# Router gathers paced by TensorE's progress, with the last three batches behind all expert tiles

## The reference, cut to what matters

```python
h = (x_flat @ W_gat).reshape(M, HEADS, NUM_EXPERTS)
e = leaky_relu(a_src[src] + a_dst[dst])            # per edge and head
ee = exp(e - segment_max(e, dst)[dst])
denom = segment_sum(ee, dst)
agg = segment_sum(h[src] * (ee / denom[dst])[:, :, None], dst)
topk_s, topk_i = top_k(layernorm(agg).mean_over_heads, 2)
w = softmax(topk_s)
for ei in range(4):                                # every expert for every node
    g = where(topk_i == ei, w, 0).sum(-1)
    out = out + g * (gelu(x @ W1[ei] + b1[ei]) @ W2[ei] + b2[ei])
```

## Time and profile before

| | |
|---|---|
| runs, median (lowest to highest) | 4270.76 us (4270.12 to 4277.53) |
| profiled execution, span | 5331.2 us |
| block 3, first matmul to the add of tile 99 | 2841.8 to 4967.6 us |
| POOL busy, whole span | 2832.6 us (53%) |
| PE busy, whole span | 3564.3 us (67%) |
| DVE busy, whole span | 2082.9 us (39%) |

### The profile page before, as it was taken

The page is one execution under the profiler, slowest core; times in us unless marked ns, Lnnn a source line. Parts: engine busy times, 40 slices in busy tenths (PEclk is TensorE's granted clock), DMA queues, the critical chain, the costliest instruction groups (busy, mean ns, idle before and its releaser), DMA issues. The chain is left out here.

```text
span 5331.2 us, 46344 instructions
## 1 busy us (share of the span) xinstructions
PE 3564.3 (67%) x12937; PEld 2313.0 (43%) x12938; DVE 2082.9 (39%) x4892; ACT 801.1 (15%) x1970; POOL 2832.6 (53%) x2937
## 2 busy tenths in 40 slices
PE   0688888888757777777626377768685777789200
PEld 0455555555445455555413154444453454455100
DVE  5456655665546555544311020211111120212378
ACT  5111211111101111111101011111111111112000
POOL 2666666666666666666655623653636444630420
PEclk9889899998878888888767588888787788899655
DMA  7444444444445555555512111211112111211387
GB/s 250 128 109 115 112 111 112 112 115 112 112 111 148 138 153 154 162 152 152 125 33 61 18 49 28 58 38 48 35 50 43 44 48 36 60 50 48 118 254 253
DMA packets 381413, 540.57 MB, mean 101 GB/s; under 512 B 120314, under 2 KB 297818, under 8 KB 381143
## 3 DMA queue, kind: packets, MB, share of 16 engines
q0 software_dynamic: 119136, 234.44, 20.0%
q1 hardware_dynamic: 243119, 288.12, 16.8%
q10 hardware_dynamic: 19016, 16.48, 0.9%
HBM read 392.03 MB, written 146.74 MB: 101 GB/s over the span
## 5 line engine op out<-in xcount | busy, mean ns | idle before, releaser
L788 POOL DMA_INDIRECT rows<-xn_rows,gsrc x1664 | 1606.6, 965 | 908.5 <-issue 459.8
L1357 POOL DMA_INDIRECT nb<-route_rows,idx x1024 | 1000.3, 977 | 897.7 <-DVE msg L1432 480.9
L1093 PE MATMUL PS<-rows,oh 128*128 128x257 f32 x3328 | 910.0, 427 | 351.9 <-issue 220.0
L1686 PE MATMUL PS<-arena,hid 128*125 128x256 f32 x3200 | 865.1, 422 | 408.5 <-issue 298.6
L1686 PEld LDWEIGHTS PS<-arena,hid 128*125 128x125 f32 x3200 | 662.9, 209 | 621.3 <-issue 502.6
L1093 PEld LDWEIGHTS PS<-rows,oh 128*128 128x128 f32 x3328 | 693.8, 214 | 488.8 <-issue 296.6
L1621 DVE TENSOR_TENSOR y_sb<-PS,b_b 125x512 f32<-125x512 f32 x200 | 128.7, 685 | 1781.4 <-remote 975.2
L1678 PE MATMUL PS<-x2g,arena 128*128 128x500 f32 x1600 | 722.6, 610 | 147.3 <-issue 94.0
L1678 PEld LDWEIGHTS PS<-x2g,arena 128*128 128x128 f32 x1600 | 313.5, 197 | 541.6 <-issue 473.0
L1647 ACT ACTIVATE hid<-PS,b_sb 128x500 f32<-128x500 f32 x400 | 269.9, 677 | 1109.9 <-PE PS L1678 688.9
L1165 PE MATMUL PS<-own_w,p_t 128*125 128x512 f32 x400 | 231.2, 662 | 77.7 <-ACT s_t L1053 54.5
(11 more groups left out here) (304 smaller groups left out, 3086.8 us busy)
## 6 DMA issues: line engine op xcount, KB each, us to landing
y_rows<-y_sb SPq DMA_DIRECT2D x100, 512.0 KB
arena<-y_rows SPq DMA_DIRECT2D x100, 512.0 KB
rows<-xn_rows,gsrc POOLq DMA_INDIRECT x1664
nb<-route_rows,idx POOLq DMA_INDIRECT x1024
sum_rows<-kept SPq DMA_DIRECT2D x104, 128.5 KB
x_rows<-x SPq DMA_DIRECT2D x100, 128.0 KB
hid<-x_rows SPq DMA_DIRECT2D x100, 128.0 KB
m_in<-sum_rows SPq DMA_DIRECT2D x100, 125.5 KB
```

Source lines behind the costliest of these rows:

```text
L788: pool.indirect_dma_start(out=rows[w][h][:, q, 0:D], out_offset=None, in_=xn_rows, in_offset=bass.IndirectOffsetOnAxis(ap=gsrc[:, s * HU + ...
L1093: last = mm(SUM[:, 0:D + 1], oh[w][h][:, q, :], rows[w][h][:, q, :], start=h == 0 and q == 0, stop=h == 1 and q == HU - 1)
L1357: pool.indirect_dma_start(out=nb[b % NBUF][:, c, :], out_offset=None, in_=route_rows, in_offset=bass.IndirectOffsetOnAxis(ap=idx[:, b * W ...
L1686: last = mm(Y[j % 2][e // 2][0:NP, (e % 2) * D:(e % 2 + 1) * D], hid[:, 4 * e + k, j * NP:(j + 1) * NP], w2_sb[:, e, k, :], start=k == 0, ...
```

## The change

Four things change together.

1. unit_after spaces the batches at 7 tiles in place of 5.65. scores(0) moves from tile 8 to 12, scores(12) from tile 76 to 96, and batches 13, 14 and 15 (LATE) get no tile: their scores and records stand behind the add of tile 99, one batch after the other.
2. Every fourth gather of a batch (SPREAD) also waits until TensorE has come to tile (b + c/64) * 7 + 1, told by s_hp in a group's first half and by s_y in its second (where_pe_is). From tile 100 on there is no such wait: the last one is that of column 8 in batch 14, which waits for 99 tiles.
3. The lane chain and its two transposes stand behind everything, no longer between tiles. The exps move with them.
4. SyncE stores the records of the late batches after it has issued the last stage's first eight tiles of loads.

```diff
@@ -49,6 +49,8 @@
 FG = NT // FT
 AHEAD = 4
 REST = 16
+SPREAD = 4
+TILES_A_BATCH = 7
 EVEN = 112
 NS = 2 * SPANS
 MIX_AT = NT + 3
@@ -150,8 +152,16 @@
 
 def unit_after(b):
 
-    t = int((b + 1) * 5.65) + 3
+    t = int((b + 1) * TILES_A_BATCH) + 3
     return t if t % 4 < 2 else t + 4 - t % 4
+
+
+def where_pe_is(tiles):
+
+    group, rest = int(tiles // 4), tiles % 4
+    if rest < 2:
+        return 0, group * 16 + int(rest * 8) + 1
+    return 1, group * 4 + int((rest - 2) * 2)
 
 
 def build(nc, x, src, dst, gnn_w, gnn_b, wqkv, wkv_t, wout_t, bout, w_gat, att_src, att_dst,
@@ -1285,8 +1295,7 @@
             s_out = [ev(f"s_out{q}") for q in range(AR)]
 
             batches_after = lambda t: [b for b in range(NB) if unit_after(b) == t]
-            LAST = unit_after(NB - 1)
-            assert LAST + 4 < NT and LAST // 4 == NG - 2
+            LATE = [b for b in range(NB) if unit_after(b) > NT - 4]
 
             @block.sync
             def _(sp):
@@ -1300,6 +1309,11 @@
                         sp.wait_ge(s_hp, (g - 1) * 16)
                     for i in range(4):
                         sp.dma_start(x2g[u][:, :, i, :], x2_turned[4 * g + i].rearrange("p (k n) -> p k n", k=2)).then_inc(s_x2l[u], 16)
+
+                def store_records(b):
+                    sp.wait_ge(s_rec, b + 1)
+                    sp.dma_start(rec_rows[0:EF, :].rearrange("(p f) c -> p f c", p=P)[:, b * W:(b + 1) * W, :],
+                                 rec[b % 2][:]).then_inc(s_recs[b % 2], 16)
 
                 load_group(0)
                 load_group(1)
@@ -1309,9 +1323,7 @@
                     sp.wait_ge(s_yc, t + 1)
                     sp.dma_start(y_rows[t], y_sb[t % 2][:]).then_inc(s_ys[t % 2], 16)
                     for b in batches_after(t - 2):
-                        sp.wait_ge(s_rec, b + 1)
-                        sp.dma_start(rec_rows[0:EF, :].rearrange("(p f) c -> p f c", p=P)[:, b * W:(b + 1) * W, :],
-                                     rec[b % 2][:]).then_inc(s_recs[b % 2], 16)
+                        store_records(b)
                     if t % 4 == 0 and t // 4 + 2 < NG:
                         load_group(t // 4 + 2)
 
@@ -1332,6 +1344,8 @@
                     sp.wait_ge(s_ys[u], 16 * NT // 2)
                 for t in range(YR):
                     final_loads(t)
+                for b in LATE:
+                    store_records(b)
                 for t in range(YR, NT):
                     final_loads(t)
                 for q in range(AR):
@@ -1349,6 +1363,10 @@
                     if b >= NBUF:
                         pool.wait_ge(s_nbf, b - NBUF + 1)
                     for c in range(W):
+                        at = (b + c / W) * TILES_A_BATCH + 1
+                        if c % SPREAD == 0 and at < NT:
+                            which, count = where_pe_is(at)
+                            pool.wait_ge((s_hp, s_y)[which], count)
                         if (b or c) and c % REST == 0:
                             for q in range(AHEAD):
                                 pool.wait_ge(s_nb[q], (b * W + c) // AHEAD * 16)
@@ -1627,9 +1645,11 @@
                         records(b)
                     for b in batches_after(t):
                         scores(b)
-                    for part, at in ((lane_ends, 1), (over_lanes, 2), (lane_sums, 3), (first_maxima, 4), (first_records, 5)):
-                        if t == LAST + at:
-                            part()
+                for b in LATE:
+                    scores(b)
+                    records(b)
+                for part in (lane_ends, over_lanes, lane_sums, first_maxima, first_records):
+                    part()
                 for k in range(FG):
                     weigh(k)
                     for t in range(k * FT, (k + 1) * FT):
@@ -1649,9 +1669,11 @@
                         for b in batches_after(4 * g + j):
                             act.wait_ge(s_dif, b + 1)
                             a(dd[:], dd[:], ACT.Exp).then_inc(s_ex, 1)
-                    if g == LAST // 4:
-                        act.wait_ge(s_endd, 1)
-                        a(dc[:], dc[:], ACT.Exp).then_inc(s_ende, 1)
+                for b in LATE:
+                    act.wait_ge(s_dif, b + 1)
+                    a(dd[:], dd[:], ACT.Exp).then_inc(s_ex, 1)
+                act.wait_ge(s_endd, 1)
+                a(dc[:], dc[:], ACT.Exp).then_inc(s_ende, 1)
                 act.wait_ge(s_fixd, 1)
                 a(d4[:], d4[:], ACT.Exp).then_inc(s_fixe, 1)
                 for k in range(FG):
@@ -1686,16 +1708,6 @@
                                 last = mm(Y[j % 2][e // 2][0:NP, (e % 2) * D:(e % 2 + 1) * D], hid[:, 4 * e + k, j * NP:(j + 1) * NP],
                                           w2_sb[:, e, k, :], start=k == 0, stop=k == 3)
                         last.then_inc(s_y, 1)
-                        if isinstance(g, int) and 4 * g + j == LAST + 2:
-                            pe.wait_ge(s_ends, 1)
-                            for k in range(4):
-                                last = nc.tensor.transpose(HP[0][0:20, k * P:(k + 1) * P], ends[:, k, :], ident)
-                            last.then_inc(s_endt, 1)
-                            pe.wait_ge(s_endc, 1)
-                        if isinstance(g, int) and 4 * g + j == LAST + 3:
-                            pe.wait_ge(s_fx, 1)
-                            nc.tensor.transpose(HP[1][:, 0:20], fm[:, 0:P], ident[0:20, 0:20])
-                            nc.tensor.transpose(HP[1][:, 20:40], fx[:, 0:P], ident[0:20, 0:20]).then_inc(s_back, 1)
 
                 for g in range(2):
                     group(g, g, 0)
@@ -1704,6 +1716,14 @@
                         group(i * 2 + (2 + u), u, i + 1)
                 for g in range(NG - 3, NG):
                     group(g, g % 2, g // 2)
+                pe.wait_ge(s_ends, 1)
+                for k in range(4):
+                    last = nc.tensor.transpose(HP[0][0:20, k * P:(k + 1) * P], ends[:, k, :], ident)
+                last.then_inc(s_endt, 1)
+                pe.wait_ge(s_endc, 1)
+                pe.wait_ge(s_fx, 1)
+                nc.tensor.transpose(HP[1][:, 0:20], fm[:, 0:P], ident[0:20, 0:20])
+                nc.tensor.transpose(HP[1][:, 20:40], fx[:, 0:P], ident[0:20, 0:20]).then_inc(s_back, 1)
 
 
 _INS = ["x", "src", "dst", "L0_gnn_weight", "L0_gnn_bias", "L0_mix_Wqkv", "kv_turned", "out_turned", "L0_mix_bout",
```

## The result

The changed kernel takes 4325.37 us (median of four runs, 4318.19 to 4328.70), the kernel before 4270.44 beside it. The ratio is 1.0122, 95% interval 1.0108 to 1.0137: some 52 us slower (55 between the two medians). The forecast had the sign right, and 4360 us.

What follows compares the result with a forecast made beforehand. POOL's chain of gathers was taken to bound the kernel, with about 100 us of slack on TensorE. Tiles -101 and tail +192 gave +91 on the median of 4271, about 4360 us; range 4315 to 4445.

Steps and rivals of the forecast that it cites:

- hold: Expert block: TensorE crawls beside bursts of gathers without a semaphore wait; seen in the first profile, predicted absent in runs.
- TensorE's slack: Expert tiles: TensorE alone needs less time than POOL's chain of gathers; about 100 us.
- The first rival: Expert block: unpaced gathers hold TensorE in the runs too, so the change is faster, about 3740 us; chance 0.11.
- the second: Graph stage: gathers are quicker in runs than in the trace, TensorE already bounds; about 4440 us; chance 0.12.
- the third: Paced gathers: the pace costs POOL more than its slack; 4560 us; chance 0.04.
- the fourth: Whole kernel: it comes out even, a hold of 190 us or so in the runs all goes; 4270 us; chance 0.05.
- the bounds worked out from rows, +83 and +100: Whole change: the sum with gathers at 1.394 us apart (+83) or 1.375 us (+100) instead of 1.385.
- the forecast's own 4330 to 4400: Whole kernel: range for the main case, POOL's chain as bound; chance 0.68.
- -101: Expert tiles: done 1402 us behind the first gather in place of 1503, as TensorE no longer waits for the router.
- +192: Tail: weigh(0) starts 217 us behind tile 99's add, where before it started 25.2 behind.
- 1.385 us a gather: Route gathers: interval between gathers in a burst, 87.2/63, used to price all 1,024 gathers.
- The sum of 4267: Kernel before: run time built from rows with POOL alone setting the pace, 2401 + 1420 + 82.8 + 363.6, against median 4270.8.

Runs made afterwards that it cites:

- e1: The kernel before, unchanged, profiled a second time: 4276.68 us, with a span of 4274.9 us.
- e2: The changed kernel without POOL's waits for TensorE, spacing of 7 tiles and late batches kept: 4240.17 us, 0.9918 of the kernel before.
- e8: The kernel before, unchanged, profiled a third time: 4273.46 us, with a span of 4271.7 us.
- e6: The changed kernel at spacing 5.65, no late batch, with the wait for TensorE on every gather instead of every fourth: 4303.52 us, ratio 1.0075.
- e4: The kernel before without the waits for all gathers to land ahead of every sixteenth: 4138.70 us, ratio 0.9687.

## Why the prediction was right, and where its size was wrong

The bound, the sign and the mechanism stand: no hold in the runs, the tiles gain TensorE's slack, the tail pays more. The first rival (a hold in the runs) fell with e1, e2 and e8, the second (quicker gathers in the runs) with e1, which lasts as long as a run, has gathers of 0.944 us and lets TensorE wait for the router, the third with e6, the fourth with the result. That 4325 lies in the stated range is owed to its margin: the bounds worked out from rows, +83 and +100, are 4354 and 4371, and the forecast's own 4330 to 4400 misses it by 5. The balance of terms, e1 against the changed kernel:

| step | as predicted | measured |
|---|---|---|
| tiles, to the add of tile 99 | -101 (1503 to 1402, from the first gather) | -148.5 (1540.8 to 1392.3, from the first matmul) |
| tile 99 to batch 15 landed | 161 | 173.4 |
| batch 15's scores and records | 13.8 | 13.7 |
| lane chain to first result gather | 12.9 | 12.7 |
| first result gather to weigh(0) | 28.9 | 26.2 |
| tile 99 to weigh(0), less before | +192 | +200.8 (225.9 less 25.1) |
| weigh(0) to the end | unchanged | -1.6 |
| sum, with -0.7 at the start | +91 | +50.0 (4324.9 less 4274.9) |

The runs differ by 52 to 55 us and these two executions by 50, since e1 lasted 6 us longer than the median of the kernel before that stood beside the changed one.

**The step that was mis-sized is the -101.** TensorE's own need was right to about a microsecond (1402 less 8.6 from the first gather to the first matmul is 1393.4, measured 1392.3). What was too short is POOL's chain in the kernel before, against which it was set: 1420 us from the first gather to batch 15's first scores instruction, where e1 has 1469.6 (2390.3 to 3859.9). The price of 1.385 us a gather was taken from a burst of 64, whose 63 intervals hold three rests; a batch has four, the fourth ahead of the next batch's first gather. So 1,024 gathers at that price hold 49 rests, and the kernel has 63; at 2.15 us the missing 14 are 30 of the 50 us. What is left is spread over later landings, longer rests and long gathers (below).

**Why the check against the median didn't show it.** The sum of 4267 lay within 0.1% of the median, and the prediction took that for proof. It was luck: by e1's rows its parts were off by up to 51 us and cancelled.

| part | in the sum | e1 |
|---|---|---|
| 1,663 graph gathers' intervals | 2079 | 2119.7 |
| last graph gather to first route gather | 192 | 140.6 |
| first route gather to batch 15's scores | 1420 | 1469.6 |
| scores to tile 99's add | 82.8 | 80.5 |
| that add to the end | 363.6 | 334.6 |

The first used the median duration of a gather, 0.946 us; the mean in e1 and in the changed kernel is 0.970, since some are longer. The second and the last were lengths read from the disturbed execution: the stretch of the earlier trace rows from weigh(0) to the end, 338.3 us, takes 309.5 in e1 and 307.9 in the changed kernel, with the same instructions. So stretches without route gathers were taken for undisturbed, and the first profile was disturbed there as well; the earlier trace rows show it for weigh(0).

**The tail's 12 us.** The prediction had 120 gathers at 1.385 us from 8.3 us ahead of the last add. POOL came some 6 us late to them (the first starts at 3789.93; 2.9 us of this is one gather of 3.86 us, at 3782.02), and its waits for landings were longer while the last stage's first loads ran. From POOL's timeline, the stretches on both sides of 3820, and the chain that ended last (start, us, what):

```profile
3782.02 3.86 POOL L1375 DMA_INDIRECT nb<-route_rows,idx  x1 [0.30 <-issue]
...
3806.03 0.94 POOL L1375 DMA_INDIRECT nb<-route_rows,idx  x1 [5.72 <-DMA nb<-route_rows,idx]
...
3790.00:3820.00 30.00, 0.00 (x0) 0.00 (x0) 14.10 (x40) 0.63 (x1) 17.22 (x18) 0.54 0.75 241
3820.00:3960.00 140.00, 0.00 (x0) 0.00 (x0) 13.14 (x38) 0.63 (x1) 95.89 (x101) 0.50 0.12 16
...
3799.36 5.88 DMA nb<-route_rows,idx
...
3826.77 2.35 DMA nb<-route_rows,idx
```

A gather lands after 5.88 us in the stretch in which DMA moves 241 GB/s, and after 2.35 in the one with 16 GB/s. The prediction had named those loads as issued "long before" and didn't ask what they run beside. That they cause the late landings is read from these rows alone; no run moved them.

## What to carry to other kernels

Compare a profile's span with the runs before reading a stretch of it; if it is far off, take a second profile before any term. A sum that meets the median is a test only when its parts are checked one by one: price a repeated operation by its mean over whole periods, not by the median or by a stretch that leaves one of the waits out. And an engine that bounds the kernel and is made to wait for another finishes later: pacing POOL would have needed something that it protects, while the cost to take away, the rests, stood on the path of the kernel before all the time.

## What the runs showed of the hardware

- One profiled execution can be far from the runs: 5331.2 us for the kernel before, then 4274.9 and 4271.7 for the same kernel. Its cause wasn't tried and stays open. Recording alone doesn't bring it, since the nine later profiles, of both kernels and their variants, lasted as long as the runs. In that one alone waits of VectorE, ScalarE and POOL end with what the profile calls remote, another core or an unknown queue (259.0 us ahead of graph gathers, 975.2 us ahead of VectorE's adds). The Trainium skill's rule that compute and DMA don't slow each other (page "SBUF — State Buffer", section "SBUF: two separate sides") agrees with e2, where TensorE's tiles take 1392.50 us beside unpaced gathers.
- A few gathers are long, and they stand beside VectorE's scans. In e1's timeline one takes 3.34 us, from inside the scans until 0.80 us behind their end; the gather ahead of it, beside the same scans, takes 0.99:

```profile
2951.44 5.31 DVE L1436 TENSOR_TENSOR_SCAN rec<-dd,rec,msg 128x64 f32<-128x64 f32 x20
...
2952.92 0.99 POOL L1357 DMA_INDIRECT nb<-route_rows,idx  x1 [0.30 <-issue]
2954.22 3.34 POOL L1357 DMA_INDIRECT nb<-route_rows,idx  x1 [0.30 <-issue]
```

  In e1, what the 1,024 gathers take above 0.944 us is 44 us in sum, 41 of it in 24 gathers at least 0.3 us too long, every one of which lies beside VectorE instructions. 36 of it is in 15 gathers, one in each batch whose record scans run beside gathers, and each of these ends 0.80 us behind the last scan. Nothing was run to show the cause. The same section of the Trainium skill says that VectorE and GpSimd share a pair of ports which an instruction of one can hold until its end. The ends of the long gathers agree with that in kind; why the earlier gathers beside the same scans are not long stays open.
- A satisfied semaphore wait on a POOL gather costs some 0.003 us (e6), a wait for all gathers to land 2.15 us (e4).
